# Second attention on one core: when GpSimd issues its gathers, and what stands behind them

## The chip, the cores and the metric

One Trainium2 chip, and of it one core. The core has four compute engines, TensorE (matmul), VectorE, ScalarE and GpSimd, and a fifth, SyncE, that here only issues DMAs. They run side by side and are ordered by semaphores alone. The metric is the device time of one execution in microseconds. Several runs of a kernel are given by their median.

## The reference

Two layers on 16 batches of 256 tokens with 128 features, in float32. Each layer is an attention and a mixture of experts, each with a layer norm ahead of it, a layer norm behind it and a residual. What matters here is the third stage, the attention of the second layer. It is windowed and global at once:

```python
def _L1_attn_ref(x, w_v, b_v, w_wqk, b_wqk, w_qk, b_qk, w_out, b_out, w_pos_embedding, pos_embedding):
    DIM = 128; HEADS = 16; HEAD_DIM = 8; WS = 64; SCALE = HEAD_DIM ** (-0.5)
    v = x @ w_v + b_v
    wq, wk = split(x @ w_wqk + b_wqk)            # windows of 64 tokens
    wattn = softmax(wq @ wk.T * SCALE + w_bias)
    q, k = split(x @ w_qk + b_qk)                # all 256 tokens
    attn = softmax(q @ k.T + g_bias)
    return (wattn @ v + attn @ v) @ w_out + b_out

x = x + _layernorm(_L0_ffn_ref(_layernorm(x)))   # stage 2: shared expert + 2 of 8 experts, by gates
x = x + _layernorm(_L1_attn_ref(_layernorm(x)))  # stage 3
```

Stage 2 leaves the outputs of its experts in device memory, grouped by expert. For each token the two rows of its two experts have to be fetched from there ("gathered"), weighted by the gates and added to the shared expert's output. This closing work of stage 2 ("mixing") is done inside stage 3, batch by batch.

## The kernel before

The program runs four stages one after the other: `first_attention`, `first_ffn`, `second_attention`, `second_ffn`. The change lies in `second_attention`. It is a loop over steps `k`, written out for each engine. A batch `b` has four steps (`NG` = 4), `r = k % 4`. A step works on one unit, which is four heads of one batch (two tiles of 128 tokens), and is pipelined: in step `k` the maxima are computed of unit `k`, the exponentials of unit `k - 2`, the outputs of unit `k - 3`. Steps with negative `k` fill the pipeline.

In each step TensorE goes through a fixed order, and nothing overtakes in it: the projection wq (r = 2), the global scores of the unit two back, the first maximum (`maxima(k, 0)`), the attended sums of the unit three back (L1136, L1140), the second maximum, the stack of keys of unit `k + 2` (transposes of `a_kt`, L1064), the third maximum, the windowed scores, the fourth maximum, the stack M of the queries, the window maximum, the transposes of the output, the stack Q, then the projections and the output projection that the step has. "Maximum" is short for a 128x512 matmul of scores (L1086) that VectorE reduces to row maxima (L1293); two PSUM banks take turns for them, so a matmul waits until VectorE has read the bank two before.

The stack of keys in step r = 2 is the first that needs the next batch's keys complete:

```python
pe.wait_ge(stacks_ready, 2 * ((k + KEYS) // NG + 1))
```

VectorE has its order too. At r = 2 it is: the two normalises of y (L1273, after `rs_y_ready` from GpSimd), the bias add of wq (L1316), the first maximum, the adds L1356 (mixing) and L1362 (residual), then the other maxima. At r = 3 it aggregates the statistics of the mixed batch (`mmv_y`) late and normalises x (L1273).

GpSimd's work in a step, in its order:

- r = 1: `mix_rstd` of x, the reciprocal root for the layer norm of the mixed x (L1471, L1473);
- each r: one gather, an indirect DMA that fetches a quarter of a batch's rows into `picked` (L1483). The four parts of batch n (two tiles, two experts) are issued at r = 1, 2, 3 of batch n - 5 and r = 0 of batch n - 4; VectorE multiplies them by the gates at r = 1 (L1376). `gathers(k)` lists the parts of a step;
- r = 3: `mix_rstd` of y; r = 2: `rstd` of x (waits for statistics that VectorE completes at the end of its step r = 2);
- each r: the copy of v for unit `k + 2` (L1500);
- r = 1: `rstd` of y, which VectorE's step r = 2 begins with;
- r = 0 and r = 1: `split`, which writes the queries and keys of the next batch as a rounded part and a residual, windowed at r = 0 and global at r = 1. It is a memset (L1455), two casts (L1456, L1458), a wait for these, and two subtractions (L1462, L1464). The last of these raises `stacks_ready`.

SyncE issues for each unit eight DMAs that spread the keys into `kpad` (L1040), once ScalarE has copied the stack of keys out of PSUM (L1221).

Of the kernel before, what the change touches and what calls it, by code (L numbers as in the profile page):

```python
# [25 lines left out]
B, S = 16, 256  # L26
TILES = B * S // P
TPB = S // P
# [852 lines left out]
def second_attention(nc, X, Z, ident, a):  # L881
# [8 lines left out]
    WINDOWED, GLOBAL = 0, 1  # L890
# [8 lines left out]
    def batch(n):  # L899
        return 0 <= n < B  # L900
# [32 lines left out]
    def d_count(k, task):  # L933
        return d_table[k, task]
# [5 lines left out]
    def gathers(k):  # L940

        found = []
        for at in range(k - 3 if k == FIRST else k, k + 1):
            n, part = (at + 3) // NG + 4, (at + 3) % NG
            if batch(n):
                found.append((n, part))
        return found
# [5 lines left out]
    with ExitStack() as ctx:  # L953
# [14 lines left out]
        picked = sb("picked", [P, 2, 2 * TPB, D])  # L968
# [46 lines left out]
        def mix_count(n, task):  # L1015

            return 9 * n + task
# [413 lines left out]
        def _(pool):  # L1431
# [12 lines left out]
                pool.wait_ge(pool_step, 1 + 2 * n + which)  # L1444
                nc.gpsimd.tensor_tensor(rs[:, :], ve[:, :], half[:, :], ALU.pow).then_inc(ready, 1)

            def split(k, n, kind, projected_by, transposed):

                heads, par = TPB * H, n % 2
                val = proj[:, par, :, :, :].rearrange("p a t (h d) -> p a (t h) d", d=HD)  # L1450
                pool.wait_ge(d_done, d_count(*projected_by))
                if n >= 2:
                    pool.wait_ge(a_full, a_count(*transposed))
                qd, kd = qt[:, par, kind, :, :], kt[:, par, kind, :, :]
                nc.gpsimd.memset(qd[:, :, SHIFT].bitcast(F32), 0.0)  # L1455
                nc.gpsimd.tensor_copy(qd[:, :, 0:2 * HD].rearrange("p n (c d) -> p n c d", c=2),  # L1456
                                      val[:, 2 * kind, :, :].unsqueeze(2).to_broadcast([P, heads, 2, HD]))
                nc.gpsimd.tensor_copy(  # L1458
                    kd[:, :, 0:4 * HD].rearrange("p n (c d) -> p n c d", c=2)[:, :, :, 0:HD],
                    val[:, 2 * kind + 1, :, :].unsqueeze(2).to_broadcast([P, heads, 2, HD])).then_inc(parts_hi, 1)  # L1460
                pool.wait_ge(parts_hi, 2 * n + kind + 1)
                nc.gpsimd.tensor_tensor(qd[:, :, 2 * HD:3 * HD], val[:, 2 * kind, :, :],  # L1462
                                        qd[:, :, 0:HD].bitcast(F32), ALU.subtract)
                nc.gpsimd.tensor_tensor(kd[:, :, HD:2 * HD], val[:, 2 * kind + 1, :, :],  # L1464
                                        kd[:, :, 0:HD].bitcast(F32), ALU.subtract).then_inc(stacks_ready, 1)

            def mix_rstd(n, stats, mv, rs, done, which):
                pool.wait_ge(mixed, mix_count(n, stats))
# [5 lines left out]

            for k in range(FIRST, LAST):
                b, r = k // NG, k % NG
                if r == 1 and batch(b + 3):
                    mix_rstd(b + 3, X_STATS, mmv_x, mrs_x, mrs_x_ready, 2)
                for n, part in gathers(k):
                    if part == 0 and batch(n - 2):  # L1480
                        pool.wait_ge(mixed, mix_count(n - 2, GATED))
                    at = n * 2 * TPB + part
                    nc.gpsimd.indirect_dma_start(picked[:, n % 2, part, :], None, a["ys"],  # L1483
                                                 bass.IndirectOffsetOnAxis(a["rows"][:, at:at + 1], 0)
                                                 ).then_inc(picked_full[n % 2], 16)
                if r == 3 and batch(b + 4):
                    mix_rstd(b + 4, Y_STATS, mmv_y, mrs_y, mrs_y_ready, 1)
                if k == FIRST:
# [20 lines left out]

                    split(k, b + 1, WINDOWED, (k - 2, "wk"), (k, "M"))  # L1510
                if r == 1 and 0 < b + 1 < B:
                    split(k, b + 1, GLOBAL, (k - 2, "k"), (k - 1, "M"))


TOK = 512
# [989 lines left out]
```

## Time and profile before

| | us |
|---|---|
| median of 3 runs | 1519.51 |
| lowest, highest | 1514.73, 1523.56 |
| profiled execution | 1523.5 |
| its span | 1521.7 |
| TensorE busy | 1330.5 |
| VectorE busy | 1143.1 |
| ScalarE busy | 968.4 |
| GpSimd busy | 748.9 |
| of it 64 gathers, mean of one 1.064 | 68.1 |

The profiled execution is one run; its times are used for the working below. The times of its rows are us from the start of the span. Second attention begins at about 757 us (first gather 757.1) and its last maximum is at 1264.4; the last gather starts at 1130.8.

### The profile page before, as it was taken

What the parts mean: (1) busy time and instruction counts of PE and PEld (TensorE: products, weight loads), DVE (VectorE), ACT (ScalarE), POOL (GpSimd) and SP (SyncE); (2) the same over time, 40 slices, a digit from 0 to 9 for tenths busy, and PEclk for the clock granted to TensorE, in tenths of its full rate; (3) what the DMA queues carried; (4) which work ended last, traced back from release to release, by engine and by line L of the source; (5) the groups of instructions that cost most, each with busy time, mean ns of one, the idle gap of its engine ahead of it and who ended that gap; (6) DMA issues with size and microseconds to landing.
All of it is one profiled execution on the core that took longest, in us unless ns stands there. A gap on an engine that the chain in (4) does not pass through costs nothing. (4 is left out here: it accounts for less than half of the span.)

```text
span 1521.7 us, 34315 instructions
## 1 busy us (share of the span) xinstructions
PE 1330.5 (87%) x12185; PEld 1007.4 (66%) x12185; DVE 1143.1 (75%) x3071; ACT 968.4 (64%) x1498; POOL 748.9 (49%) x962
## 2 busy tenths in 40 slices
PE   2899999999997687999639999999999996899996
PEld 1566666666654465899626767776777774788885
DVE  5578888888866455999757788888888775576765
ACT  1688888888875355777705666766777775334341
POOL 5776656877833342999675444454453221001111
PEclk9799999999999689999958999999999998899998
DMA  6000000111110120222222111111111110000000
GB/s 228 15 23 21 21 22 19 29 32 30 33 33 25 39 66 10 61 76 71 77 67 53 44 45 45 46 45 45 46 44 40 40 40 5 1 1 14 7 14 21
DMA packets 75101, 60.68 MB, mean 40 GB/s; under 512 B 17088, under 2 KB 71104, under 8 KB 74560
## 3 DMA queue, kind: packets, MB, share of 16 engines
q1 hardware_dynamic: 70848, 50.21, 12.3%
q0 software_dynamic: 4096, 8.40, 1.9%
q8 instruction: 95, 1.56, 0.4%
q14 instruction: 62, 0.51, 0.1%
HBM read 20.01 MB, written 13.37 MB: 22 GB/s over the span
## 5 line engine op out<-in xcount | busy, mean ns | idle before, releaser
L541 ACT ACTIVATE a_p<-a_ps_s 128x1024 f32<-128x1024 f32 x256 | 258.3, 1031 | 25.1 <-PE a_ps_s L400 21.5
L651 DVE TENSOR_REDUCE a_qt<-a_ps_d 128x2 fp32r<-128x512 f32 x256 | 174.6, 688 | 47.3 <-PE a_ps_d L411 42.7
L1293 DVE TENSOR_REDUCE a_qt<-a_ps_d 128x2 fp32r<-128x512 f32 x256 | 172.5, 689 | 49.5 <-PE a_ps_d L1086 44.7
L822 POOL TENSOR_TENSOR a_rn<-a_ss,a_half 128x16 f32<-128x16 f32 x56 | 162.6, 2921 | 1.3
L1086 PE MATMUL a_ps_d<-a_kpad,a_qs 128*128 128x512 f32 x256 | 127.2, 499 | 18.8 <-DVE a_qt L1293 11.2
L1203 ACT ACTIVATE a_pg<-a_ps_s 128x1024 f32<-128x1024 f32 x128 | 125.8, 1024 | 27.2 <-PE a_ps_s L1075 25.6
L418 PE MATMUL a_ps_o<-a_p,a_v 128*32 128x256 f32 x2048 | 128.6, 391 | 3.8 <-ACT a_p L541 3.7
L411 PE MATMUL a_ps_d<-a_kpad,a_qs 128*128 128x512 f32 x256 | 127.0, 496 | 3.6 <-DVE a_qt L651 3.0
L2229 ACT ACTIVATE f_s<-f_ps_g 128x512 f32<-128x512 f32 x72 | 42.9, 598 | 96.6 <-PE f_ps_g L2167 88.4
L418 PEld LDWEIGHTS a_ps_o<-a_p,a_v 128*32 128x32 f32 x2048 | 61.0, 111 | 53.1 <-issue 22.2
L1992 DVE TENSOR_TENSOR f_sl<-f_s,f_sh 128x512 fp32r<-128x512 f32 x78 | 77.8, 1037 | 8.2 <-ACT f_sh L1880 8.2
L1064 PE MATMUL a_ps_a<-ident,a_qt 128*128 128x128 f32 x512 | 80.6, 281 | 1.2 <-ACT a_kc L1221 0.8
L190 POOL DMA_INDIRECT xs<-Z,r_at x64 | 68.2, 1066 | 24.0 <-issue 15.5
L1086 PEld LDWEIGHTS a_ps_d<-a_kpad,a_qs 128*128 128x128 f32 x256 | 48.6, 191 | 47.3 <-DVE a_qt L1293 16.3
L1225 ACT CAST a_qsm<-a_ps_a 128x512 fp32r<-128x512 f32 x64 | 37.5, 586 | 62.3 <-PE a_ps_a L1064 60.7
L411 PEld LDWEIGHTS a_ps_d<-a_kpad,a_qs 128*128 128x128 f32 x256 | 48.3, 189 | 39.7 <-issue 11.2
L1483 POOL DMA_INDIRECT a_picked<-ys,rows x64 | 68.1, 1064 | 13.0 <-issue 12.1
L2278 DVE TENSOR_TENSOR f_p<-f_h,f_ps_x 128x512 f32<-128x512 f32 x64 | 43.8, 685 | 34.1 <-PE f_ps_x L2139 32.0
L1136 PE MATMUL a_ps_o<-a_pg,a_v 128*32 128x256 f32 x1024 | 68.5, 385 | 0.4 <-ACT a_pw L1229 0.4
L2152 PEld LDWEIGHTS f_ps_y<-wd,f_p 128*128 128x128 f32 x512 | 65.3, 191 | 4.1 <-DVE f_p L2278 0.4
L1064 PEld LDWEIGHTS a_ps_a<-ident,a_qt 128*128 128x128 f32 x512 | 61.2, 144 | 8.8 <-issue 6.1
L2152 PE MATMUL f_ps_y<-wd,f_p 128*128 128x128 f32 x512 | 66.3, 275 | 0.2 <-DVE f_p L2278 0.2
(359 smaller groups left out, 3898.7 us busy)
## 6 DMA issues: line engine op xcount, KB each, us to landing
a_kpad<-a_kc SPq DMA_DIRECT2D x512, 32.0 KB
a_kpad<-a_kq SPq DMA_DIRECT2D x256, 32.0 KB, 1.8
f_xin<-xs SPq DMA_DIRECT2D x39, 128.0 KB, 2.1
ys<-f_yout SPq DMA_DIRECT2D x39, 128.0 KB, 2.1
w<-in_w SPq DMA_DIRECT2D x2, 2304.0 KB, 11.3
out_x<-X SPq DMA_DIRECT2D x8, 256.0 KB, 2.3
xs<-f_zero SPq DMA_DIRECT2D x15, 128.0 KB
wgu<-in_wgu SPq DMA_DIRECT2D x1, 1152.0 KB
```

Of the source, the lines that this page charges most:

```text
L411: nc.tensor.matmul(bank(st.k, f"m{part}")[:, :], qs2[:, (st.k - 1) % 2, t * P:(t + 1) * P], kpad[:, u % PAD_RING, 2 * c:2 * c + 2, :].rear ...
L418: last = nc.tensor.matmul(ps_o[SLOT * j:SLOT * (j + 1), half * S:(half + 1) * S], v32[:, u % V_RING, t, j, :], probs[:, u % 2, j, t, :], s ...
L541: nc.scalar.activation(probs[:, u % 2, 2 * c:2 * c + 2, :, :].rearrange("p a b c -> p (a b c)"), ps_s[:, 2 * c:2 * c + 2, :].rearrange("p ...
L651: nc.vector.tensor_reduce(qt2[:, (k - PEAK) % 4, 2 * part:2 * part + 2, SHIFT], bank(k, f"m{part}")[:, :].rearrange("p (a b) -> p a b", b= ...
L822: nc.gpsimd.tensor_tensor(rn[:, part * c:(part + 1) * c], ss[:, part * c:(part + 1) * c], half[:, 0:c], ALU.pow).then_inc(rn_ready, 1)
L1064: last = nc.tensor.transpose(ps_a[:, n:n + P], stacked(src[:, (u // NG) % 2, kind, t * H + t0:t * H + t0 + G, :]), ident[:, :])
L1086: nc.tensor.matmul(bank(k, f"m{part}")[:, :], qs[:, k % 2, t * P:(t + 1) * P], kpad[:, k % PAD_RING, GLOBAL, 2 * c:2 * c + 2, :].rearrange ...
L1136: nc.tensor.matmul(ps_o[SLOT * j:SLOT * (j + 1), 0:S], v32[:, u % V_RING, t, j, :], pg[:, u % 2, j, t, :], start=t == 0, stop=t == TPB - 1)
L1203: nc.scalar.activation(pg[:, u % 2, 2 * c:2 * c + 2, :, :].rearrange("p a b c -> p (a b c)"), ps_s[:, 2 * c:2 * c + 2, :].rearrange("p a b ...
L1293: nc.vector.tensor_reduce(qt[:, b % 2, GLOBAL, n:n + 2, SHIFT], bank(k, f"m{part}")[:, :].rearrange("p (j s) -> p j s", s=S), AX.X, ALU.ma ...
L1992: nc.vector.tensor_tensor(sl[:, half_of(n, h)], s[:, half_of(n, h)], sh[:, half_of(n, h)].bitcast(F32), ALU.subtract).then_inc(sl_done, 1)
L2152: last = nc.tensor.matmul(ps_y[:, t * D:(t + 1) * D], src, a["wd"][:, q * D:(q + 1) * D], start=q == 0 and t == 0, stop=q == NQ - 1 and t ...
```

## The change

The gathers go into a function `gather(k)`. Each now also waits for the first maximum of its own step (the semaphore `d_full`, raised by TensorE), where the step has one. At r = 0 and r = 1 the gather stands ahead of GpSimd's other work of the step. At r = 2 GpSimd begins with the gather of the next step, r = 3. The gather of step r = 2 itself is issued from within the global `split` of step r = 1, between the casts and the residuals; where there is no such split (while the pipeline fills, and at the end) it is issued at the start of r = 2.

```diff
@@ -1444,7 +1444,7 @@
                 pool.wait_ge(pool_step, 1 + 2 * n + which)
                 nc.gpsimd.tensor_tensor(rs[:, :], ve[:, :], half[:, :], ALU.pow).then_inc(ready, 1)
 
-            def split(k, n, kind, projected_by, transposed):
+            def split(k, n, kind, projected_by, transposed, between=None):
 
                 heads, par = TPB * H, n % 2
                 val = proj[:, par, :, :, :].rearrange("p a t (h d) -> p a (t h) d", d=HD)
@@ -1458,11 +1458,26 @@
                 nc.gpsimd.tensor_copy(
                     kd[:, :, 0:4 * HD].rearrange("p n (c d) -> p n c d", c=2)[:, :, :, 0:HD],
                     val[:, 2 * kind + 1, :, :].unsqueeze(2).to_broadcast([P, heads, 2, HD])).then_inc(parts_hi, 1)
+                if between is not None:
+                    gather(between)
                 pool.wait_ge(parts_hi, 2 * n + kind + 1)
                 nc.gpsimd.tensor_tensor(qd[:, :, 2 * HD:3 * HD], val[:, 2 * kind, :, :],
                                         qd[:, :, 0:HD].bitcast(F32), ALU.subtract)
                 nc.gpsimd.tensor_tensor(kd[:, :, HD:2 * HD], val[:, 2 * kind + 1, :, :],
                                         kd[:, :, 0:HD].bitcast(F32), ALU.subtract).then_inc(stacks_ready, 1)
+
+            def gather(k):
+
+                for n, part in gathers(k):
+                    if part == 0 and batch(n - 2):
+                        pool.wait_ge(mixed, mix_count(n - 2, GATED))
+                    if d_live(k, "m0"):
+
+                        pool.wait_ge(d_full, d_count(k, "m0"))
+                    at = n * 2 * TPB + part
+                    nc.gpsimd.indirect_dma_start(picked[:, n % 2, part, :], None, a["ys"],
+                                                 bass.IndirectOffsetOnAxis(a["rows"][:, at:at + 1], 0)
+                                                 ).then_inc(picked_full[n % 2], 16)
 
             def mix_rstd(n, stats, mv, rs, done, which):
                 pool.wait_ge(mixed, mix_count(n, stats))
@@ -1474,15 +1489,14 @@
 
             for k in range(FIRST, LAST):
                 b, r = k // NG, k % NG
+                if r < 2:
+                    gather(k)
+                if r == 2:
+                    if not 0 < b + 1 < B:
+                        gather(k)
+                    gather(k + 1)
                 if r == 1 and batch(b + 3):
                     mix_rstd(b + 3, X_STATS, mmv_x, mrs_x, mrs_x_ready, 2)
-                for n, part in gathers(k):
-                    if part == 0 and batch(n - 2):
-                        pool.wait_ge(mixed, mix_count(n - 2, GATED))
-                    at = n * 2 * TPB + part
-                    nc.gpsimd.indirect_dma_start(picked[:, n % 2, part, :], None, a["ys"],
-                                                 bass.IndirectOffsetOnAxis(a["rows"][:, at:at + 1], 0)
-                                                 ).then_inc(picked_full[n % 2], 16)
                 if r == 3 and batch(b + 4):
                     mix_rstd(b + 4, Y_STATS, mmv_y, mrs_y, mrs_y_ready, 1)
                 if k == FIRST:
@@ -1509,7 +1523,7 @@
 
                     split(k, b + 1, WINDOWED, (k - 2, "wk"), (k, "M"))
                 if r == 1 and 0 < b + 1 < B:
-                    split(k, b + 1, GLOBAL, (k - 2, "k"), (k - 1, "M"))
+                    split(k, b + 1, GLOBAL, (k - 2, "k"), (k - 1, "M"), k + 1)
 
 
 TOK = 512
```

## Rows read from the trace of the kernel before

**Rows 1.** Windows: nine batches, then single steps; busy time by engine, PEclk, DMA.
```profile
core 0: us, PE busy (x) PEld busy (x) DVE busy (x) ACT busy (x) POOL busy (x), PEclk, DMA share, GB/s
858.72:1129.62 270.90, 256.64 (x2849) 191.48 (x2845) 231.54 (x602) 189.72 (x307) 134.18 (x234) 1.00 0.19 45
880.82:888.85 8.03, 7.54 (x87) 5.60 (x83) 5.50 (x18) 5.40 (x9) 2.52 (x5) 1.00 0.19 45
903.05:910.90 7.85, 6.80 (x81) 4.96 (x77) 7.72 (x18) 5.15 (x8) 3.15 (x4) 1.00 0.19 45
1122.01:1129.62 7.61, 7.52 (x87) 5.61 (x83) 5.55 (x18) 5.50 (x9) 2.52 (x5) 1.00 0.18 45
1172.27:1178.96 6.69, 6.69 (x81) 5.04 (x77) 5.95 (x15) 5.14 (x8) 0.30 (x1) 1.00 0.19 44
1178.96:1186.28 7.32, 7.32 (x86) 5.69 (x83) 5.18 (x15) 5.47 (x9) 1.54 (x5) 1.00 0.18 43
841.65:851.38 9.73, 8.22 (x76) 6.51 (x76) 5.95 (x13) 5.07 (x8) 3.09 (x4) 0.82 0.19 47
812.90:820.53 7.63, 6.53 (x44) 5.01 (x40) 5.30 (x10) 4.68 (x7) 4.17 (x6) 0.78 0.24 61
```

**Rows 2.** Timeline of step r = 2, batch 3: start, length, engine, line, [idle before].
```profile
903.70 1.59 DVE L1273 TENSOR_SCALAR a_y<-a_y,a_mv_y,a_rs_y 128x128 f32<-128x128 f32 x2
904.48 0.73 POOL L1464 TENSOR_TENSOR a_kt<-a_proj,a_kt 128x256 fp32r<-128x256 f32 x1
905.68 0.50 PE L1086 MATMUL a_ps_d<-a_kpad,a_qs 128*128 128x512 f32 x1 [0.72 <-DVE a_proj L1316]
905.81 0.57 PEld L1064 LDWEIGHTS a_ps_a<-ident,a_kt 128*128 128x128 f32 x4
907.55 0.50 PE L1086 MATMUL a_ps_d<-a_kpad,a_qs 128*128 128x512 f32 x1 [0.33 <-DVE a_qt L1293]
```

**Rows 3.** Timeline of step r = 3, and of one without a gather.
```profile
912.64 1.08 POOL L1483 DMA_INDIRECT a_picked<-ys,rows  x1 [0.18 <-issue]
912.76 0.51 PE L1086 MATMUL a_ps_d<-a_kpad,a_qs 128*128 128x512 f32 x1
913.86 0.44 PE L1075 MATMUL a_ps_s<-a_qsm,a_kc 32*128 32x128 f32 x8
914.15 1.98 DVE L1293 TENSOR_REDUCE a_qt<-a_ps_d 128x2 fp32r<-128x512 f32 x3 [1.64 <-PE a_ps_d L1086]
914.90 0.50 PE L1086 MATMUL a_ps_d<-a_kpad,a_qs 128*128 128x512 f32 x1 [0.59 <-DVE a_qt L1293]
...
1152.76 0.50 PE L1086 MATMUL a_ps_d<-a_kpad,a_qs 128*128 128x512 f32 x1
1153.30 2.18 DVE L1293 TENSOR_REDUCE a_qt<-a_ps_d 128x2 fp32r<-128x512 f32 x3 [0.78 <-PE a_ps_d L1086]
```

**Rows 4.** Timeline of steps r = 2 of batches 0 and 1.
```profile
814.99 0.66 PE L1064 MATMUL a_ps_a<-ident,a_kt 128*128 128x128 f32 x4 [0.45 <-POOL a_kt L1464]
...
840.54 1.06 POOL L1462 TENSOR_TENSOR a_qt<-a_proj,a_qt 128x256 fp32r<-128x256 f32 x1
```

**Rows 5.** Timeline of step r = 0, around its gather.
```profile
889.77 0.60 DVE L1273 TENSOR_SCALAR a_mix<-a_mix,a_mmv_y,a_mrs_y 128x128 f32<-128x128 f32 x2
889.98 1.08 POOL L1483 DMA_INDIRECT a_picked<-ys,rows  x1 [0.18 <-issue]
891.07 0.32 POOL L1500 COPY a_v<-a_vt 128x64 f32<-128x64 f32 x1
```

**Rows 6.** Timeline and window of batch 1, r = 2.
```profile
846.54 0.50 PE L1086 MATMUL a_ps_d<-a_kpad,a_qs 128*128 128x512 f32 x1 [1.51 <-DVE a_qt L1293]
...
848.00:851.00 3.00, 3.00 (x21) 2.88 (x19) 1.47 (x4) 1.90 (x4) 0.00 (x0) 0.60 0.23 55
```

**Rows 7.** Timeline of GpSimd, step r = 1.
```profile
898.41 0.22 POOL L1471 TENSOR_SCALAR a_mve<-a_mmv_x 128x2 f32<-128x2 f32 x1 [2.29 <-DVE a_mmv_x L1284]
```

**Rows 8.** The fill: timeline of GpSimd, and waits from 757 to 800 us.
```profile
776.67 0.24 POOL L1471 TENSOR_SCALAR a_mve<-a_mmv_y 128x2 f32<-128x2 f32 x1
...
DVE a_mix L1273 <- POOL a_mrs_y L1473: 8.2, 3, 4.8
```

## The prediction

> **What bounds the kernel now.** TensorE is busy for 1330.5 of 1521.7 us, but the change touches second attention alone, so the windows of that stage come first. From 858.72 to 1129.62 us nine batches run in 270.90 us, 30.1 each, with TensorE busy for 95% and the clock at 1.00 [rows 1]. Then the windows of single steps, cut at the matmul of each first maximum [rows 1]. The step with r=3 (880.82) takes 8.03 us and holds 7.54 us of TensorE; r=2 (903.05) takes 7.85 and holds 6.80. The same two steps behind the last gather (1178.96 and 1172.27) take 7.32 and 6.69 us, all of it TensorE. So about 0.7 us of r=3 and 1.16 us of r=2 are waits, and only those can be won; r=1 has none and r=0 little.
>
> The timeline of r=2 shows its wait [rows 2]. VectorE's two normalises of y take 1.59 us, 0.8 each, beside GpSimd's residuals; the same shape takes 0.60 for two elsewhere [rows 5]. The bias add of wq stands behind them, and so the second maximum starts at 905.68, 2.63 us into the step, after a wait of 0.72. Its free place is 1.86 us, as in r=3 (912.76, a step that began at 910.90).
>
> The timeline of r=3 shows the other [rows 3]. The second maximum runs from 912.76 to 913.27, but VectorE, idle for 1.64 us, reduces it only at 914.15, which is 0.43 us behind the end of a gather (912.64 + 1.08), and the fourth maximum waits 0.59 us for that. Without a gather (1152.76 + 0.50 to 1153.30) the reduction follows by 0.04 us. Of the 18 steps r=3 and r=0 of this stretch that have a gather, 17 have the reduction 0.3 to 0.6 us behind the gather's end; the one without that wait, at 1122.01, takes 7.61 us [rows 1]. I read this as a signal from TensorE that comes late while a gather is issued. The trace shows the coincidence, not the mechanism.
>
> **The change, part by part.** No work is added: 64 gathers stay 64, at some 1.07 us each. What changes is when they start, and what stands behind them.
>
> *r=3, a gain.* Its gather is issued from r=2 and waits for the first maximum of r=3, which ends at 911.4. It is now ahead of the rstd of x and the copy of v, which pushed it to 912.64. It would run from 911.6 to 912.7 and be over before the second maximum ends. The reduction then starts at about 913.3 and the fourth maximum at 914.3, behind the windowed scores (913.86 + 0.44), in place of 914.90 [rows 3]: 0.56 us. The undisturbed steps bound it: 8.03 − 7.61 = 0.4 and 8.03 − 7.32 = 0.7 [rows 1]. Eight such steps (batches 2 to 9): −4.5 us, between −3.1 and −5.5. What is now behind the gather, rstd of x and v, is covered: x is normalised only at the end of r=3, and v is read three steps later.
>
> *r=2, a loss that eats the relief.* The second split's residuals now wait for a gather, and that for the first maximum of r=2, which starts at 903.05 and ends at 903.5. Gather 903.7 to 904.77, then residuals of 0.73 us 0.7 apart (as 904.48 [rows 2]), end 906.2. TensorE's stack of the next batch's keys needs them. Its weights were loaded at 905.81 and would be at about 906.25, 3.2 us into the step. That this wait can bind is seen once, at 814.99 [rows 4]. Y is normalised free of residuals and the second maximum comes at 1.9 us, but it stands ahead of the stack in TensorE's order, so the 0.7 us won are waited away behind it. From that weight load to the next step took 910.90 − 905.81 = 5.09 us, of which 0.33 was a wait of the fourth maximum [rows 2] that falls away: 4.76. The step is then 3.2 + 4.8 = 8.0 us where it was 7.85: +0.15.
>
> To this comes contention: VectorE's adds L1356 and L1362 now fall on the first residual. Beside VectorE's work a residual took between 0.73 (904.48) and 1.06 us (840.54) [rows 2, 4], so 0 to 0.33 more. I take 0.2, between the two, since here both start at one time. Together +0.35 us on nine steps (batches 2 to 10): +3.2, between +0.8 and +4.5.
>
> The Trainium skill speaks against this place. "SBUF — State Buffer", section "SBUF: two separate sides", says that a VectorE instruction in a two-port mode, which a tensor_scalar can be ("Who interferes with whom"), keeps GpSimd from writing descriptors until it ends. By it the gather would end some 0.2 us later behind y's normalise, an estimate, and nine steps would cost 2 us more. The trace has that meeting: a tensor_scalar pair from 889.77 to 890.37 over a gather from 889.98 that took 1.08 us, no more than others [rows 5]. I go by the row.
>
> *Batches 0 and 1, r=2.* Here no rstd separates two gathers, and both fall into r=2. In batch 1 TensorE waits 1.51 us for a reduction behind the second one and its clock falls to 0.60 [rows 6]; the step takes 9.73 us [rows 1]. The second gather now leaves the step, the wait of the stack comes in. From 8.0 + 0.5 us: −1.2, or +0.3 if the clock still falls. Batch 0 had the stack 2.1 us into the step (814.99 after 812.90) and gets it at 3.2 or more, in a step whose clock was 0.78 anyway [rows 1, 4]: +0.8, between +0.4 and +1.5.
>
> *r=1 and r=0.* In r=1 the gather moves ahead of the rstd of x, into the 2.29 us in which GpSimd waited for that rstd's input until 898.41 [rows 7]. Nothing waited for what stands behind: 0. It would cost 1.25 us of GpSimd's time if that idle stretch were gone. In r=0 the gather starts 1.1 us into the step (889.98), behind the rstd of y issued in r=3; the new wait is over by then: 0.
>
> *The fill.* r=1's gather is now issued while the rstd of x still waits, and part 2's ahead of the splits. At 776.67 the rstd of y starts straight behind a gather, with no wait of its own; VectorE waited for such an rstd three times, 8.2 us in total [rows 8]. A gather takes 1.25 us with its gap, and one goes from ahead of that rstd. Projections, splits and the loads of keys hang on the same chain, so the first step comes about 1.2 us earlier, and the last of the three waits gives up to 0.8 more. I take −1.5, between 0 (if the loads of keys start no earlier) and −2.0.
>
> **Sum**, against the profiled execution (1523.5 us, span 1521.7): −4.5 + 3.2 − 1.2 + 0.8 − 1.5 = −3.2, so 1520.3. That execution is 4.0 above the median of the three runs, 1519.51; in their terms 1516.3 us. The terms' ends, not all at once, give the forecast's own range of 1512 to 1523. A measurement of this kernel tells about 0.5% (7.6 us) from no change.
>
> **Rivals.**
> 1. *The reduction in r=3 stays late*, for a reason other than the gather, or behind it wherever it stands. For: the exception at 1122.01. Against: 17 of 18. Then −4.5 falls away: 1520.8 us, no change to be measured.
> 2. *Slower: the clock falls in r=2.* TensorE's wait there becomes one piece, from the end of the second maximum (2.4 us) to 3.2 or 3.5. A wait of 0.72 left the clock at 1.00; one of 1.51 was followed by 0.60 [rows 2, 6]. Behind the latter the fourth maximum was 4.84 us ahead of the next step (846.54 to 851.38) where 3.35 is usual (907.55 to 910.90): +1.5. On nine steps 13.5 us: 1529.8. Against it: the step's sum of waits hardly grows. It decides if the wait in one piece gets near 1.5 us, so if the residuals end 3.9 us into the step.
> 3. *Faster: r=2 nears its free 6.69 us.* If the stack didn't wait, the loss of 3.2 would go and 1.16 x 9 = 10.4 us come in: 1502.7. For: VectorE is busy for 7.72 of the 7.85 us of r=2 [rows 1], and 1.4 of that would be freed. Against: GpSimd's next instruction starts only where a gather ends (891.07 behind 889.98 + 1.08 [rows 5]), so the residuals can't be ready 2.0 us into the step.
>
> **Chances.** Forecast 0.62; rival 1 0.17; rival 2 0.09; rival 3 or a part of it (r=0 gains too, the fill gives more) 0.12. The range takes in the forecast and rival 1, leaves out most of rivals 2 and 3, and adds some 3 us for the scatter of medians (1514.73 to 1523.56 before): 1508 to 1526. Faster by over 0.5%: rival 3 and the low end of the forecast, 0.17. Slower: rival 2 and a small tail, 0.10. Within 0.5%: 0.73.
>
> **What would show it.** Right: r=3 steps near 7.4 us with the second maximum's reduction 0.04 us behind its matmul; r=2 steps near 8.2, y's normalises at 0.3 us each, and TensorE's stack of keys waiting 0.7 to 1.1 us for L1464; r=0 and r=1 as before; the first maximum at 797.5 in place of 798.87. Wrong: r=3 still near 8.0 (rival 1), a clock below 1 in every r=2 (rival 2), r=2 below 7.5 (rival 3).

## The result

The kernel after takes 1524.39 us (median of 18 executions, 1519.65 to 1527.51), the kernel before 1519.36 on the same chip (18 executions, 1512.78 to 1523.56). The ratio is 1.0033, 95% interval 1.0021 to 1.0045: slower by 5.0 us, inside the 0.5% band, but not the small gain forecast. The profiled execution has a span of 1521.9 us and a time of 1523.65, next to 1521.7 and 1523.5 before.

The windows of the kernel after, with the columns of [rows 1]. In order: r=2 of batches 3, 5, 7, 0 and 1, then r=3, r=1 and the same nine batches.

```profile
901.04:909.22 8.18, 6.89 (x81) 5.00 (x77) 6.98 (x18) 5.20 (x8) 2.79 (x3) 1.00 0.18 44
961.03:970.59 9.56, 8.26 (x80) 6.57 (x76) 7.19 (x18) 5.27 (x8) 2.79 (x3) 0.82 0.19 44
1022.35:1033.19 10.84, 8.32 (x80) 6.08 (x77) 6.56 (x18) 5.27 (x8) 3.04 (x3) 0.84 0.16 38
809.26:819.73 10.47, 7.94 (x44) 6.10 (x40) 5.11 (x9) 4.69 (x7) 2.59 (x3) 0.67 0.19 47
841.33:849.25 7.92, 6.80 (x81) 4.98 (x77) 5.91 (x13) 5.21 (x8) 2.61 (x3) 1.00 0.16 41
909.22:916.55 7.33, 7.33 (x86) 5.67 (x82) 5.56 (x18) 5.43 (x9) 2.45 (x5) 1.00 0.20 49
894.07:901.04 6.97, 6.90 (x78) 4.95 (x78) 5.91 (x18) 5.27 (x9) 4.27 (x9) 1.00 0.20 47
...
856.57:1130.88 274.31, 260.33 (x2849) 194.08 (x2845) 224.35 (x602) 190.01 (x307) 130.78 (x234) 0.99 0.19 45
```

The nine batches take 274.31 us where they took 270.90 [rows 1]. r=3 has gone from 8.03 to 7.33, all of it TensorE. r=2 has gone from 7.85 to 8.18, and two of its nine steps are longer still, at clocks of 0.82 and 0.84. r=1 has gone from 6.69 to 6.97, which the sum had at zero.

The timeline of r=2, batch 3, in the kernel after (the counterpart of [rows 2]); L1478 is the gather, L1464 and L1466 are the residuals.

```profile
901.28 0.60 DVE L1273 TENSOR_SCALAR a_y<-a_y,a_mv_y,a_rs_y 128x128 f32<-128x128 f32 x2
...
901.80 1.08 POOL L1478 DMA_INDIRECT a_picked<-ys,rows  x1 [2.03 <-PE a_ps_d L1086]
...
902.88 0.50 PE L1086 MATMUL a_ps_d<-a_kpad,a_qs 128*128 128x512 f32 x1
902.91 0.85 POOL L1464 TENSOR_TENSOR a_qt<-a_proj,a_qt 128x256 fp32r<-128x256 f32 x1
903.09 0.94 DVE L1362 TENSOR_TENSOR X<-X,a_y 128x256 f32<-128x256 f32 x1
903.72 0.90 POOL L1466 TENSOR_TENSOR a_kt<-a_proj,a_kt 128x256 fp32r<-128x256 f32 x1
...
904.68 0.66 PE L1064 MATMUL a_ps_a<-ident,a_kt 128*128 128x128 f32 x4 [1.29 <-POOL a_kt L1466]
905.09 0.48 PE L1086 MATMUL a_ps_d<-a_kpad,a_qs 128*128 128x512 f32 x1
```

The step is as predicted. The y-normalises take 0.60 us in place of 1.59, and the second maximum comes 1.84 us into the step. But GpSimd stood still for 2.03 us before the gather, the residuals end at 904.62, and TensorE waits 1.29 us for them with nothing to do.

The timeline of r=3 after (the counterpart of [rows 3]): the gather is over at 910.97, the second maximum follows, and its reduction starts 0.04 us behind it.

```profile
910.00 0.97 POOL L1478 DMA_INDIRECT a_picked<-ys,rows  x1 [5.37 <-PE a_ps_d L1086]
...
911.09 0.51 PE L1086 MATMUL a_ps_d<-a_kpad,a_qs 128*128 128x512 f32 x1
...
911.64 2.16 DVE L1293 TENSOR_REDUCE a_qt<-a_ps_d 128x2 fp32r<-128x512 f32 x3 [0.80 <-PE a_ps_d L1086]
```

The timeline of r=1 after: its gather now lies over the second maximum (895.91 to 896.42), and the late reduction, 0.37 us behind, has moved in with it.

```profile
895.30 1.01 POOL L1478 DMA_INDIRECT a_picked<-ys,rows  x1 [1.45 <-PE a_ps_d L1086]
...
895.91 0.51 PE L1086 MATMUL a_ps_d<-a_kpad,a_qs 128*128 128x512 f32 x1
...
896.79 1.98 DVE L1293 TENSOR_REDUCE a_qt<-a_ps_d 128x2 fp32r<-128x512 f32 x3 [0.60 <-PE a_ps_d L1086]
```

The ledger, that is the change of each stretch between the starts of first maxima. First maximum of the stage 798.87 to 796.35: −2.5. From it to the third step: 14.03 to 12.91, −1.1. Steps 2 to 7: 45.82 to 47.31, +1.5. Nine batches: +3.4, made of r=2 +7.0, r=1 +2.8, r=0 −0.7 and r=3 −5.6. Behind: −0.1 to the last maximum and −1.0 to the end. The sum is +0.2 between the two profiled executions. Of the first −2.5, 1.6 was there already at the stage's first gather (757.07 to 755.51), before anything that the change touches. The executions vary by more than this sum, so the 5.0 us between the medians has to be explained with more runs.

### The profile page after: what moved, and what is told of

The parts are those of the page before. It is cut to its first block and busy times, and to the rows that moved or that the text cites. A ratio compares the mean times of both kernels' runs of the same rounds, so it can differ in the third digit from the quotient of the medians.

```text
span 1521.9 us, 34326 instructions
## 1 busy us (share of the span) xinstructions
PE 1332.2 (88%) x12185; PEld 1007.1 (66%) x12185; DVE 1134.8 (75%) x3071; ACT 968.7 (64%) x1498; POOL 745.4 (49%) x962
## 5 line engine op out<-in xcount | busy, mean ns | idle before, releaser
L1478 POOL DMA_INDIRECT a_picked<-ys,rows x64 | 67.0, 1048 | 113.6 <-PE a_ps_d L1086 103.2
```

## The experiments

Every kernel below is timed against the kernel before on its own chip. **Two kinds of chip came up.** On one, the kernel before takes 1497 to 1498 us ("quick chip"; numbers 8 and 5 in the record, each met twice); on the other, 1519 to 1522 us ("first chip": the pair above, whose chip has no number in the record, and chip 13 with e7, e8_split_first and e6_again). That the difference belongs to the chip is the plain reading, not a tested one. The step tables differ between them, and that turned out to matter. A step is cut from one first maximum's matmul to the next; the medians are over batches 2 to 10.

| kernel | ratio to before, 95% | r=0 | r=1 | r=2 | r=3 | r=2 of batch 0, 1 |
|---|---|---|---|---|---|---|
| before, first chip | 1 | 7.54 | 6.70 | 7.85 | 8.01 | 7.63, 9.73 |
| after, first chip | 1.0033 (1.0021 to 1.0045) | 7.50 | 6.98 | 8.19 | 7.33 | 10.47, 7.92 |
| b_again, quick (before) | one execution | 7.37 | 6.70 | 7.85 | 7.33 | 6.45, 6.60 |
| a_again, quick (after) | 1.0066 (1.0045 to 1.0087) | 7.36 | 6.89 | 8.19 | 7.33 | 9.99, 7.92 |
| e1_no_between, quick | 0.9931 (0.9908 to 0.9954) | 7.37 | 6.89 | 7.03 | 7.32 | 5.65, 6.59 |
| e2_r3_only, quick | 1.0002 (0.9989 to 1.0015) | 7.37 | 6.69 | 7.85 | 7.32 | 6.44, 6.59 |
| e3_between_only, quick | 1.0062 (1.0036 to 1.0088) | 7.36 | 6.70 | 8.17 | 7.33 | 8.96, 7.90 |
| e4_r1_only, quick | 0.9961 (0.9948 to 0.9974) | 7.36 | 6.89 | 7.03 | 7.33 | 5.63, 6.60 |
| e5_between_no_wait, quick | 0.9997 (0.9983 to 1.0011) | 7.36 | 6.89 | 7.83 | 7.32 | 7.74, 6.60 |
| e6_no_waits, quick | 0.9938 (0.9918 to 0.9958) | 7.36 | 6.70 | 7.03 | 7.33 | 6.02, 6.59 |
| e6_again, first chip's kind | 0.9927 (0.9914 to 0.9941) | 7.52 | 6.70 | 7.66 | 7.33 | 6.04, 6.58 |
| e7_longer_gap, first chip's kind | 1.0111 (1.0082 to 1.0139) | 7.51 | 7.00 | 8.78 | 7.33 | 10.72, 10.08 |
| e8_split_first, first chip's kind | 0.9887 (0.9872 to 0.9902) | 7.51 | 6.70 | 6.84 | 7.32 | 6.10, 6.60 |
| e8_again, quick | 0.9885 (0.9866 to 0.9903) | 7.36 | 6.70 | 6.66 | 7.33 | 5.64, 6.59 |

### Each part of the change by itself

**e1_no_between** is the kernel after with the gather of r=2 behind the residuals, at the start of r=2:

```diff
-                if r < 2:
+                if r < 3:
                     gather(k)
                 if r == 2:
-                    if not 0 < b + 1 < B:
-                        gather(k)
                     gather(k + 1)
...
-                    split(k, b + 1, GLOBAL, (k - 2, "k"), (k - 1, "M"), k + 1)
+                    split(k, b + 1, GLOBAL, (k - 2, "k"), (k - 1, "M"))
```

> The changed kernel, but the gather of step r = 2 is issued at the start of r = 2, behind the residuals and still after the first maximum; the new places at r = 0, 1 and 3 stay. Theory A (the loss sits in r = 2: residuals wait behind a gather, TensorE's stack of keys waits for them in one piece, and the clock falls in some of these steps): the residuals end about 1 us ahead of y's normalises, which take 0.6 us for two; r = 2 steps take 6.7 to 7.0 us in place of 8.18, r = 3 stays at 7.33, r = 1 at 6.98, no clock below 1.00 in the steps of batches 2 to 10; about 12 us below before, 1505 to 1510 us. Theory B (moving the gathers ahead at r = 0, 1, 3 costs by itself, the place between casts and residuals does little): still slower than before, 1520 us or more.

Measured: 0.9931, 9.4 us faster than before where after is slower. r=2 takes 7.03 us, and no clock falls in the nine steps: theory A.

**e2_r3_only** is before with the gather of r=3 alone hoisted into r=2, behind r=2's own, waiting for r=3's first maximum (hold):

```diff
...                                       # the gather moved into gather(k, hold=True)
+                if not (r == 3 and unit(k)):
+                    gather(k, False)      # hold=False: no wait
+                if r == 2 and unit(k + 1):
+                    gather(k + 1)
```

> The kernel before, with one part of the change: in the steps that have a unit, the gather of r = 3 is issued at the start of GpSimd's step r = 2 work's second place, behind the gather of r = 2, and waits for the first maximum of r = 3; all others as before. Theory A (a gather delays the signal of TensorE's second maximum in r = 3): the reduction follows its matmul by 0.04 us, r = 3 takes 7.33 us in place of 8.0, r = 2 and r = 1 as before (7.85, 6.70), 5 us below before. Theory B (the reduction in r = 3 is late for another reason and came on time in the changed kernel because r = 2 had changed): r = 3 stays near 8.0 and the time does not move.

Measured: 1.0002. r=3 was 7.32 us, but there was nothing to win: e3 and e4 leave that gather in its old place and have 7.33 as well. So the run decides nothing between A and B. It ran twice more, for the reason below:

> The kernel of e2_r3_only once more: before, but with r=3's gather alone hoisted into r=2. Theory K (the late reduction of the second maximum under a gather shows on chips where before takes 1520 us, and not on those where it takes 1497): on a chip of 1520 us, r=3 steps 8.0 to 7.33, 4.5 to 6 us gained, ratio 0.996 to 0.997; on a chip of 1497 us, ratio 0.999 to 1.001 as before. Theory L (the late reduction was a matter of the profiled execution): ratio 0.999 to 1.001 on either chip.

> The kernel of e2_r3_only, to meet a chip where before takes 1520 us. There, theory K: r=3 steps 8.0 to 7.33 and a ratio of 0.996 to 0.997; theory L: 0.999 to 1.001. On a chip of 1497 us both say 0.999 to 1.001, and nothing is told apart.

Both met a quick chip: 0.9992 (0.9981 to 1.0002) and 1.0002 (0.9988 to 1.0016), so K and L aren't told apart.

**e3_between_only** is before with the gather of r=2 alone between casts and residuals, with its wait:

> The kernel before, with one part of the change: the gather of r = 2 stands between casts and residuals of the split at r = 1 and waits for the first maximum of r = 2; all others as before. Theory A: y's normalises take 0.6 us for two, TensorE's stack of keys waits 1.3 us or more for the last residual, r = 2 takes 8.2 to 8.4 us in place of 7.85, r = 3 stays at 8.0, the clock falls in one to four r = 2 steps at 1.4 us or more each: 4 to 12 us above before. Theory B (the place between costs nothing much and r = 1 and the fill carry the loss): within 3 us of before.

Measured: 1.0062, 11.3 us slower, two clock falls in the nine steps. That is theory A for r=2; r=3 was 7.33 and not the 8.0 that A expected. Repeated:

> The kernel of e3_between_only once more (before, with r=2's gather alone between casts and residuals, r=3's in its old place). On a chip of 1520 us, theory K: r=3 steps stay at 8.0, r=2 8.2 with one to three clock falls, ratio 1.006 to 1.009, that is 0.003 to 0.005 above after's 1.0033. Theory L: r=3 7.33. On a chip of 1497 us 1.005 to 1.008.

Again a quick chip, 1.0076 (1.0047 to 1.0106), r=2 8.17 with two longer steps, r=3 7.33.

**e4_r1_only** is before with the gather of r=1 alone ahead of the square root of x, with its wait:

```diff
+                if r == 1 and unit(k):
+                    gather(k)
                 if r == 1 and batch(b + 3):
                     mix_rstd(b + 3, X_STATS, mmv_x, mrs_x, mrs_x_ready, 2)
...
+                if not (r == 1 and unit(k)):
+                    gather(k, False)
```

> The kernel before, with one part of the change: in the steps that have a unit, the gather of r = 1 stands ahead of the rstd of x and waits for the first maximum; all others as before, so the residuals come 1.2 us earlier. Theory A: r = 1 takes 6.98 in place of 6.70 us, since the second maximum's reduction now comes 0.4 us behind the gather. In r = 2 the residuals end before y's normalises, which take 0.6 us for two; but the gather of r = 2 now runs over the end of the first maximum and delays its reduction to about 1.9 us into the step, so r = 2 takes 7.2 to 7.7 us in place of 7.85. Sum: 0 to 4 us below before. Theory B (a gather delays no signal): r = 1 stays at 6.70 and r = 2 goes to 6.7 to 6.9, 9 us or more below before.

Measured: 0.9961, 7.1 us faster, between what A and B expected; r=2 falls to 7.03, below A's range, and r=1 grows to 6.89, which B had at 6.70. Repeated:

> The kernel of e4_r1_only once more: before, but with r=1's gather alone ahead of the square root of x. Theory K: on a chip of 1520 us the r=3 steps stay at 8.0 (their gather stands in its old place), r=2 goes from 7.85 to 7.0, r=1 is 6.9 to 7.0, ratio 0.995 to 0.997. Theory L: r=3 7.33, and the rest the same.

Measured, quick chip: 0.9938 (0.9919 to 0.9957), the same steps.

So the relief of r=2 doesn't come from r=2's own gather. In before, r=1's gather stood behind the square root of x and pushed the residuals into r=2, under the y-normalises. Taken out of that place it gives 0.82 us in each r=2. The gather between casts and residuals takes this back and 0.3 us more, whether r=1's is moved (a_again 8.19) or not (e3 8.17).

### The two kernels on the quick chip

> The kernel before, unchanged, for its step table on the chip of these runs. Theory A (the late reduction of the second maximum in r=3 comes of where the gather stands): r=3 steps of 8.0 us again, with the reduction 0.4 us or more behind its matmul. Theory B (it belongs to the chip or the execution, since the kernels with the gather in its old place showed 7.33 on the second chip): r=3 steps of 7.33 if this is the second chip. r=2 steps of 7.85 by both; the r=2 steps of batches 0 and 1 at 6.4 and 6.6 by B, 7.6 and 9.7 by A.

> The kernel after, unchanged, against before on the chip of these runs. Theory A (r=3 gives back 4 to 5 us, r=2 takes 3 and the clock falls take the rest): ratio 1.002 to 1.005 as before. Theory B (r=3 gives nothing where the reduction isn't late, r=1 ahead of the square root gives about 7 us in r=2 that the gather between casts and residuals more than takes back): by the single-part runs 8.17 - 7.85 = 0.32 us for each of nine r=2 steps and two to three steps with a clock fall of 1 to 2 us, batch 0's step 2.5 us longer, batch 1's 1.3 longer, r=1 1.7 us longer: 1.004 to 1.008. r=2 steps 8.17 median by both.

Measured: before 1496.09 (one execution), after 1.0066, 10.2 us slower: theory B for both. From b_again to a_again the ledger is: r=2 +7.0, r=1 +1.7, steps 2 to 7 +4.7, the fill −3.2, the rest 0: +10.1 to the last maximum. Of the −3.2, 1.4 was there at the stage's first gather (742.55 to 741.10), so the change gave 1.8; behind the last maximum a_again's execution is 1.5 us longer, which no part of the change explains. The term of r=3 is absent. Here is why: the r=3 step of b_again. These are the very places of [rows 3], the gather 1.75 us into the step and the second maximum 0.12 behind it.

```profile
891.91 0.62 PE L1140 MATMUL a_ps_o<-a_pw,a_v 128*32 128x128 f32 x16
892.34 1.07 POOL L1483 DMA_INDIRECT a_picked<-ys,rows  x1 [0.18 <-issue]
892.46 0.51 PE L1086 MATMUL a_ps_d<-a_kpad,a_qs 128*128 128x512 f32 x1
892.60 0.59 ACT L1218 COPY a_ot<-a_ps_o 128x512 f32<-128x512 f32 x1
...
893.00 2.17 DVE L1293 TENSOR_REDUCE a_qt<-a_ps_d 128x2 fp32r<-128x512 f32 x3 [0.79 <-PE a_ps_d L1086]
```

And the two rows of the kernel before on the first chip that [rows 3] left out:

```profile
912.21 0.62 PE L1140 MATMUL a_ps_o<-a_pw,a_v 128*32 128x128 f32 x16
...
913.44 0.59 ACT L1218 COPY a_ot<-a_ps_o 128x512 f32<-128x512 f32 x1 [0.47 <-PE a_ps_o L1140]
```

On the quick chip the reduction starts at 893.00, 0.03 us behind its matmul, while the gather is still running. On the first chip it starts 0.88 us behind its matmul. ScalarE's copy is late there too: 1.23 us behind the start of its matmuls, against 0.69. TensorE's own matmuls start at the same places. So on that kind of chip both engines that read what TensorE has written get going late beside a gather. On the other kind neither does, but for one step among the 117 of r=3 in its thirteen traces (e4_r1_only, batch 8: 7.43 us, the reduction 0.18 us late and the copy 0.47).

### The place or the wait

**e5_between_no_wait** is the kernel after, but the gather in between doesn't wait:

```diff
                 if between is not None:
-                    gather(between)
+                    gather(between, False)
```

> The kernel after, but the gather that stands between casts and residuals doesn't wait for the first maximum (all the others do as in after). Theory W (the harm is the wait, which holds the two residuals until the first maximum begins, while the place costs only the gather's own 1.0 us): the residuals end 1.5 to 2 us sooner in r=2, the wait for the stack of keys is gone, r=2 steps 7.0 to 7.9 us, no clock falls, ratio 0.993 to 0.999. Theory P (the place does it: any gather ahead of the residuals pushes them into the y-normalises and the reductions): r=2 steps stay near 8.2, ratio 1.003 to 1.007.

Measured: 0.9997 (a tenth execution of 2438.72 us is not in it); no clock below 1.00 in the nine steps, and TensorE never waits for the residuals in them. But r=2 takes 7.83 us, not 7.03. The timeline of e5:

```profile
911.68 1.32 POOL L1478 DMA_INDIRECT a_picked<-ys,rows  x1 [0.17 <-issue]
...
913.03 0.85 POOL L1464 TENSOR_TENSOR a_qt<-a_proj,a_qt 128x256 fp32r<-128x256 f32 x1
...
913.85 0.73 POOL L1466 TENSOR_TENSOR a_kt<-a_proj,a_kt 128x256 fp32r<-128x256 f32 x1
913.89 1.03 DVE L1273 TENSOR_SCALAR a_y<-a_y,a_mv_y,a_rs_y 128x128 f32<-128x128 f32 x2
...
915.31 0.50 PE L1086 MATMUL a_ps_d<-a_kpad,a_qs 128*128 128x512 f32 x1 [0.72 <-DVE a_proj L1316]
```

Both theories hold in part. The place alone costs the relief: the residuals run to 914.58, the y-normalises meet them, and the second maximum waits 0.72 us, as in [rows 2]. The wait costs the rest: a further 0.36 us a step, the clock falls and 2.3 us in batch 0. In batch 1 it costs 1.3 us (7.92 against 6.60). Against e1 the place costs 0.0066 of the time, the wait 0.0069.

**e6_no_waits** is e1_no_between without any wait for a first maximum.

> The kernel with all gathers first in their steps and none between (as e1_no_between), but without any wait for the first maximum. Theory P (only the place matters: GpSimd is idle there): r=1 6.9, r=2 7.0, r=3 7.33, ratio 0.992 to 0.996, that of e1_no_between. Theory H (the wait is what helps, as it keeps the gather's descriptor writing clear of VectorE's work before the maximum): r=1 and r=3 0.2 to 0.7 us longer, ratio 0.997 to 1.003.

Measured: 0.9938, level with e1: theory P. The waits for the maxima buy nothing on this chip, and in r=1 they cost: 6.89 with, 6.70 without. Why, in two timelines. First e4_r1_only, with the wait:

```profile
906.14 0.61 POOL L1458 CAST a_kt<-a_proj 128x512 fp32r<-128x512 f32 x1
906.42 0.88 DVE L1376 TENSOR_TENSOR a_mix<-a_picked,gates 128x512 f32<-128x512 f32 x1
```

Then e6_no_waits:

```profile
904.83 0.61 POOL L1458 CAST a_kt<-a_proj 128x512 fp32r<-128x512 f32 x1
...
905.33 0.68 DVE L1376 TENSOR_TENSOR a_mix<-a_picked,gates 128x512 f32<-128x512 f32 x1
```

The gate multiply that starts with 0.33 us of the cast still to run takes 0.20 us more; with 0.11 left it takes its usual 0.68. Those 0.20 us are the 0.19 of the step: the next first maximum waits for what VectorE does behind the multiply (a_both, 0.16). The Trainium skill ("SBUF — State Buffer", section "SBUF: two separate sides") says that GpSimd and VectorE share a port pair, and that whichever starts first keeps it for the whole instruction. It names VectorE instructions with two SBUF inputs beside a GpSimd instruction that reads SBUF, which is the case here. The trace agrees in direction and not in size: the multiply lost 0.20 us over a cast with 0.33 to run, and the add L1362 of the kernel after took 0.94 us for 0.41 over a residual, where a block until the end of GpSimd's instruction would have made them 0.13 and 0.14 us longer still.

### Does the gap's length set the clock fall?

**e7_longer_gap** is the kernel after with a filling of zeros (128x1024) behind the gather in between.

```diff
+        idle = sb("idle", [P, 1024])
...
                     gather(between)
+                    nc.gpsimd.memset(idle[:, :], 0.0)
```

> The kernel after with a filling of zeros of 128x1024 behind the gather that stands between casts and residuals, so that TensorE's wait for the stack of keys in r=2 grows from 1.3 us by the filling's length, estimated at 0.6 to 1.2 us from the 0.61 us of a cast of 128x512. Theory G (a clock fall follows the length of this gap: none to two in nine steps at 1.3 us, and in every step seen with 2.5 us): a clock fall of 1.3 to 1.8 us in most of the nine r=2 steps, so steps of 10.0 to 11.0 us, total of batches 2 to 10 longer than after's by 15 to 25 us, ratio to before 1.018 to 1.028. Theory C (falls come by chance or from the rest of the program, whatever the gap): two or three falls as in after, steps of 8.8 to 9.4 us, 6 to 11 us longer than after, ratio 1.010 to 1.014.

Measured: 1.0111, on the first chip's kind: by the ratios 12 us more than after (by the medians, 13.7 and 5.0 above before, 9 us), within theory C's range. The windows of r=2 of batches 4, 7 and 8:

```profile
937.03:945.80 8.77, 6.88 (x80) 4.99 (x76) 6.50 (x18) 5.20 (x8) 3.41 (x4) 1.00 0.15 38
1029.08:1040.75 11.67, 8.26 (x81) 6.57 (x77) 6.67 (x18) 5.27 (x8) 3.96 (x4) 0.85 0.15 35
1062.60:1072.80 10.20, 8.31 (x81) 6.07 (x77) 6.60 (x18) 5.28 (x8) 3.40 (x4) 0.83 0.16 40
```

The filling made TensorE's gap 1.89 us where it was 1.29, and each r=2 longer by 0.59, one for one. Seven of the nine steps kept a clock of 1.00. Theory G, that the fall follows from the gap's length, is wrong at this length: what the longer gap costs in most steps is its own length. Whether falls become more frequent the few steps can't say. Counted over the kernels with this gap: at 1.3 us the clock fell in 5 of 32 steps (after, a_again, e3 and e3_again; eight each), at 1.9 us in 3 of 11 (e7 with its batch 1, and batch 7 of e3 and e3_again), at 2.5 us and more in all three seen (batch 7 of after, a_again and e7), and with no gap for the stack (e5) in none of nine. A fall costs 9.56 − 8.18 = 1.4 us.

Batch 7 stands apart. Its step in the kernel after:

```profile
1024.09 1.63 POOL L1478 DMA_INDIRECT a_picked<-ys,rows  x1 [2.98 <-issue]
...
1026.43 0.73 POOL L1466 TENSOR_TENSOR a_kt<-a_proj,a_kt 128x256 fp32r<-128x256 f32 x1
1027.21 0.66 PE L1064 MATMUL a_ps_a<-ident,a_kt 128*128 128x128 f32 x4 [2.52 <-POOL a_kt L1466]
```

The gather starts 1.74 us into the step where others start at 0.76, and ends on nothing that the profile shows. a_again, e3, e3_again and e7 have it in the same step; in e5 the gather there starts 0.33 us later than in other batches. Placed ahead of the residuals with the wait, this hiccup lengthens TensorE's gap by 0.65 us (e3: 1.95 for 1.29) to 1.5 us (e7: 3.41 for 1.89). In the order of e1 it costs nothing that shows.

### A better order

**e8_split_first** is e6_no_waits with the casts and residuals of r=1 right behind the gather:

```diff
+                if r == 1 and 0 < b + 1 < B:
+                    split(k, b + 1, GLOBAL, (k - 2, "k"), (k - 1, "M"))
                 if r == 1 and batch(b + 3):
                     mix_rstd(b + 3, X_STATS, mmv_x, mrs_x, mrs_x_ready, 2)
...
-                if r == 1 and 0 < b + 1 < B:
-                    split(k, b + 1, GLOBAL, (k - 2, "k"), (k - 1, "M"))
```

> The kernel of e6_no_waits with the casts and residuals of r=1 right behind the gather, ahead of the square root of x, the copy of v and the square root of y. Theory R (what remains of r=2's length over 6.69 us, and the y-normalises' 1.6 us in before, is the overlap of the residuals with VectorE's gate multiply and y-normalises): the residuals are over before the gate multiply, L1464 and L1466 take 0.73 us each, r=2 goes from 7.03 to 6.7 or less, 3 to 4 us gained, ratio to before 0.990 to 0.993. Theory S (the casts and residuals then overlap the reductions of the maxima and delay x's square root): r=1 grows by 0.3 or more and the ratio is 0.994 to 0.998.

> The kernel of e6_no_waits once more, for the pair with e8_split_first on one chip. Expected by every theory: ratio 0.992 to 0.996; r=1 6.70, r=2 7.03, r=3 7.33 if it is the second chip. If it is the first chip: r=3 8.0 (the gather of r=3 stands in r=2 here and is over before the second maximum, so 7.33 by the theory that a gather under the second maximum delays its reduction there).

> The kernel of e8_split_first once more. On a chip of 1520 us: 0.987 to 0.991 as before. On a chip of 1497 us, where nothing is to be had in r=3: r=2 6.7 to 6.85, r=1 6.70, 1484 to 1487 us, ratio 0.990 to 0.993.

Measured: e8 0.9887 on the first chip's kind (1504.22 us) and 0.9885 on a quick one (1481.53 us), 17 us faster than before on both, and more than was expected of either. In the traces of the quick chip the stage, from first gather to last maximum, went from 494.6 us (b_again) to 479.8. The timeline of GpSimd and VectorE at the end of r=1 in e8_again, and the window of its r=2:

```profile
902.90 0.73 POOL L1466 TENSOR_TENSOR a_kt<-a_proj,a_kt 128x256 fp32r<-128x256 f32 x1
...
905.10 0.71 POOL L1445 TENSOR_TENSOR a_rs_y<-a_ve,a_half 128x2 f32<-128x2 f32 x1
905.32 0.68 DVE L1376 TENSOR_TENSOR a_mix<-a_picked,gates 128x512 f32<-128x512 f32 x1
```

```profile
906.63:913.29 6.66, 6.66 (x80) 5.01 (x76) 6.42 (x18) 5.15 (x8) 1.40 (x2) 1.00 0.23 59
```

The residuals end at 903.63, 1.7 us before the gate multiply, neither that nor the y-normalises meet them, and r=2 is all TensorE: 6.66 us, the free step of [rows 1].

e6_again shows the first chip's kind once more. This order has no gather over the second maximum of r=1 or r=3, and both steps are free: 6.70 and 7.33. It has two gathers in r=2, and that step takes 7.38 to 8.05 us where the quick chip has 7.03. The two in r=2, e6_again:

```profile
926.56 1.13 POOL L1475 DMA_INDIRECT a_picked<-ys,rows  x1 [0.16 <-issue]
...
927.99 1.43 POOL L1475 DMA_INDIRECT a_picked<-ys,rows  x1 [0.30 <-issue]
...
929.54 0.49 PE L1086 MATMUL a_ps_d<-a_kpad,a_qs 128*128 128x512 f32 x1 [0.59 <-DVE a_qt L1293]
```

The fourth maximum waits 0.59 us here, as in [rows 3]. And e8_split_first shows that a gather need not lie over the second maximum for that. Its r=2 takes 6.84 us where the quick chip has 6.66:

```profile
898.89 0.96 POOL L1475 DMA_INDIRECT a_picked<-ys,rows  x1 [0.30 <-issue]
...
899.99 0.51 PE L1086 MATMUL a_ps_d<-a_kpad,a_qs 128*128 128x512 f32 x1
...
900.80 0.59 ACT L1218 COPY a_ot<-a_ps_o 128x512 f32<-128x512 f32 x1 [0.63 <-PE a_ps_o L1140]
900.83 1.29 DVE L1293 TENSOR_REDUCE a_qt<-a_ps_d 128x2 fp32r<-128x512 f32 x2 [0.25 <-PE a_ps_d L1086]
```

The gather is over at 899.85, 0.14 us before the second maximum begins. Still the reduction starts 0.33 us behind its matmul, with VectorE idle for 0.25, and ScalarE's copy waits 0.63.

## Why the prediction went wrong

**What was right.** *r=3*, on this kind of chip: the step became 7.33 us with the reduction 0.04 to 0.09 us behind its matmul; over nine steps it gave 5.6 us where 4.5 was forecast for eight. *r=2's ordinary step*: 8.2 us forecast, 8.18 measured. The relief of the y-normalises was waited away behind the second maximum, in one piece of 1.29 us for the stack of keys, as told, though the name of the wait is L1466, and the wait was forecast at 0.7 to 1.1. That the sum met 8.18 so closely is in part luck, since two errors cancel: the residuals ended 3.58 us into the step where 3.35 was forecast (3.15 and 0.2), and from there to the next step it took 4.6 us where 4.8 was. The prediction's 4.8 had been counted from a weight load at 905.81 that ran under the second maximum, 0.21 us ahead of its own matmul; behind the wait load and matmul start together. *Contention of the residuals*: 0.12 + 0.17 us on the two, 0.3 where 0.2 was taken. *Batch 1*: −1.2 forecast, −1.8 measured. *The fill*: −1.5 forecast; the first maximum comes 2.5 us sooner, but 1.7 of that was there already at the stage's first gate multiply (764.25 against 765.96), so the change gave 0.8 there and 1.1 up to the third step, 1.9 in all, within the range of 0 to −2.0.

**What failed.** The sum was −3.2, the measured difference +5.0, and three terms make it.

1. *"Together +0.35 us on nine steps (batches 2 to 10): +3.2"* for r=2. It was +7.0 in the profile. The ordinary steps gave 9 x 0.33 = 3.0; the rest is two steps with a lower clock, one at an ordinary gap of 1.30 us (+1.4), one behind a late gather (+2.7). The prediction had this as rival 2, but as all or nothing, decided at 1.5 us. The runs show a chance instead, about one in six at 1.3 us. As a term it would have been 9 x 0.16 x 1.4, about +2.0, plus batch 7.
2. *"Nothing waited for what stands behind: 0."* for r=1. It cost 2.8 us. On the quick chip it is 0.19 a step (the cast that runs into the gate multiply), on the first chip 0.28. The gather now lies over the second maximum of r=1 (895.30 to 896.31 over 895.91 to 896.42), and on the first chip's kind, and only there, the reduction then starts 0.36 to 0.69 us behind it. The prediction named this mechanism for r=3 and didn't ask it of the step into which another gather was moved.
3. *Batch 0, "+0.8, between +0.4 and +1.5"*: +2.8. The gap grew to 2.5 us and the clock of the step fell from 0.78 to 0.67. e3 has 8.96 and e5 7.74 in this step, so place and wait both go into it.

These three are +3.8, +2.8 and +2.0 more than forecast, 8.6 us; r=3, r=0, batch 1, the fill and the stretch behind the stage gave some 5 beyond the forecast, which leaves the +0.2 of the profiled pair for the −3.2. The rest of the way to +5.0 is between executions: the profiled one of before lay 4.1 us above its kernel's median, that of after 0.7 below. On the quick chip the pair is 10.2 us apart by medians and 10.1 by the ledger up to the last maximum. There too the closeness is partly luck, as 1.4 us ahead of the stage and 1.5 behind it have nothing to do with the change; but the terms of r=2 and of batches 0 and 1 are far larger than these.

**What had been taken from one execution.** The r=3 gain belongs to a kind of chip. Where it isn't to be had, the same change costs 10 us, not 5. Rows of batches 0 and 1 of before (7.63 and 9.73 us, clocks 0.78 and 0.82) were taken as the kernel's; on the quick chips those steps take 6.45 and 6.60 us, so the −1.2 of batch 1 is a +1.3 there.

**The rivals.** Rival 1 didn't come on the first chip. Rival 2 came in part. Rival 3, r=2 at its free 6.69 us, was rejected rightly for this order; e8 shows that the 10.4 us priced for it are there, at 6.66 us a step, once the residuals are early and not late. The port rule weighed in the prediction (0.2 us more for the gather behind the y-normalises) was hardly tested: the gather started 0.76 us into the step, where 0.65 was forecast, and so lay over the normalises for their last 0.08 us only; it took 1.08 us like the others.

**What stays open.** That a gather over the second maximum makes the reduction late on the first chip's kind rests on the traces taken there (before, after, e6_again, e7, e8_split_first), in which the reduction in r=1 and r=3 is 0.36 us or more late where a gather lies over the second maximum, with one exception in before (1122.01, 0.10), and 0.15 at most where none does, and on the thirteen traces from quick chips, where one step is late. It isn't the whole rule, since r=2 of e8_split_first is late behind a gather that has ended. The direct test, e2 on the first chip's kind, is missing, as both repeats ran on quick chips; the mechanism is not shown. Why batch 7's gather starts late is open too.

## What to carry to other kernels

Ask of a move not only what it frees but which other instructions it now lies over, step by step, with the same rule everywhere: where a gather over one maximum goes with a late reduction, ask the same of the next one. On a queue that runs in order, never put a wait for the consumer's engine ahead of work that the same engine needs soon; here the gather's reader didn't mind where in the step it stood (e1, e6 and e8), the residuals' reader did. And take a step table from more than one execution before you price a wait. A stall in one piece is worth more than its length: price the chance of a clock fall as a term of the sum.

## What was not expected of the hardware

- Chips of two kinds: 1497 and 1520 us for one kernel, at much the same granted clock (0.957 and 0.947 in the profiled executions). Between the two profiled executions of before, 14.5 of the 27.4 us lie ahead of second attention's first gather (757.07 against 742.55) and stay unexplained. In this stage the difference of 12.7 us shows as readers of TensorE's results that start late beside a gather: in r=3 of before the reduction by 0.76 to 0.95 us in eight of nine steps (8.01 against 7.33 us), in r=0 by 0.1 to 0.4 (7.5 against 7.37).
- The clock fell in 5 of 32 steps with the same 1.3 us gap and in 3 of 11 with 1.9 us: at these lengths the runs give a frequency, not a rule. Behind the gap in the step at 961.03 of the kernel after, with the columns of [rows 1]:

```profile
964.67:966.70 2.03, 2.03 (x17) 1.70 (x18) 0.99 (x2) 0.59 (x1) 0.00 (x0) 0.91 0.02 4
967.00:969.00 2.00, 2.00 (x11) 2.00 (x11) 1.29 (x5) 1.51 (x2) 0.00 (x0) 0.50 0.21 49
```

  The granted clock of 0.50 in the second row is 1.2 GHz. The 0.91 of the first puts the fall at about 966.3 (an estimate: 0.37 us at half clock in 2.03 us), 1.7 us after TensorE is back at work, not in the gap itself.
- A gather over VectorE's two adds L1356 and L1362 took 1.43 us in e6_again, and 1.32 over the gate multiply and the add behind it in e5, against 0.95 to 1.08 with nothing of the kind; over a pair of normalises it took 1.07 to 1.13. Not every such meeting costs: over the add L1390 alone it took 1.08 in e8_again.
